# Turning the quantised input of a feed-forward block by transposing DMA transfers instead of TensorE transposes, in a fused macaron block

## The reference

```python
def ffn(x):                                   # weights w_gate, w_up (704 x 256), w_down (256 x 704)
    gate, y = fp4_linear(x, w_gate), fp4_linear(x, w_up)
    return fp4_linear(silu(gate) * y, w_down)
# fp4_linear: both operands quantised in blocks of 16 to the grid 0, .5, 1, 1.5, 2, 3, 4, 6
#             times a scale per block, then einsum('bsk,nk->bsn')
x = x + 0.5 * ffn(layernorm(x))               # A
x = x + scan_block(layernorm(x))              # S: 16 states for each of the 256 channels
x = x + 0.5 * ffn(layernorm(x))               # C
```

## Time and profile before

| | |
|---|---|
| median of 3 runs | 4089.68 us (4085.27 to 4096.99) |
| profiled execution, its own time | 4087.75 us |
| its span | 4085.6 us |
| lies around the span | 2.15 us |
| TensorE busy, share of the span | 3666.8 us, 90% |
| VectorE busy | 3519.3 us, 86% |
| ScalarE busy | 3020.7 us, 74% |
| GpSimd busy | 2700.2 us, 66% |
| mean granted TensorE clock | 0.962 |

### The profile page before, as it was taken

How to read it: one execution, slowest core, us unless ns; L and a number is a source line. 1 busy time by engine, 2 the same in 40 slices (tenths; PEclk the granted TensorE clock), 3 DMA queues, 4 the chain that set the end, 5 groups by cost and what they waited for, 6 DMA issues and landing times. The chain is left out here.

```text
span 4085.6 us, 81699 instructions
## 1 busy us (share of the span) xinstructions
PE 3666.8 (90%) x29740; PEld 2764.4 (68%) x29740; DVE 3519.3 (86%) x5974; ACT 3020.7 (74%) x5991; POOL 2700.2 (66%) x2163
## 2 busy tenths in 40 slices
...
GB/s 29 11 11 17 6 17 12 17 17 17 11 13 12 17 17 17 17 6 17 12 17 17 17 6 17 12 17 17 17 17 6 12 17 16 17 17 6 12 12 11
DMA packets 46452, 57.93 MB, mean 14 GB/s; under 512 B 7463, under 2 KB 41704, under 8 KB 46056
## 3 DMA queue, kind: packets, MB, share of 16 engines
q1 hardware_dynamic: 46056, 52.72, 3.9%
...
...
## 5 line engine op out<-in xcount | busy, mean ns | idle before, releaser
L803 DVE TENSOR_TENSOR_SCAN state<-w_ps,decay 128x512 f32<-128x512 f32 x1024 | 1211.4, 1211 | 31.2 <-PE w_ps L1192 20.1
L1126 PE MATMUL gu_ps<-wgu,qxT 128*128 128x352 f16 x6144 | 1064.1, 324 | 181.9 <-DVE hid L730 139.4
L1126 PEld LDWEIGHTS gu_ps<-wgu,qxT 128*128 128x128 f16 x6144 | 579.4, 100 | 616.9 <-DVE hid L730 188.3
L1192 PE MATMUL w_ps<-bdif,x_parts 128*128 128x129 f16 (+1 forms) x12288 | 846.5, 221 | 24.6 <-DVE state L803 21.1
L1192 PEld LDWEIGHTS w_ps<-bdif,x_parts 128*128 128x128 f16 x12288 | 767.2, 98 | 98.6 <-issue 53.2
L813 DVE SCALAR_TENSOR_TENSOR c_state<-state,inv_A,rep_ps 128x512 f32<-128x512 f32 x1024 | 726.4, 736 | 13.8 <-PE y_ps L1212 10.1
L1133 PE MATMUL td_ps<-wd,qhT 128*128 128x256 f32 x3072 | 728.6, 388 | 4.2 <-ACT qhT L926 4.2
L1005 ACT ACTIVATE decay<-dt,A_sb 128x512 f32<-128x512 f32 x1024 | 679.0, 714 | 4.9 <-DVE state L803 3.1
L995 ACT ACTIVATE bdif<-dif,B_tok 128x129 f16<-128x129 f16 x2048 | 637.3, 397 | 5.2 <-PE w_ps L1192 1.0
L1133 PEld LDWEIGHTS td_ps<-wd,qhT 128*128 128x128 f32 x3072 | 575.7, 194 | 78.5 <-ACT qhT L926 6.8
L926 ACT COPY qhT<-td_ps 128x256 f32<-128x256 f32 x768 | 282.0, 367 | 443.4 <-PE td_ps L1107 438.4
...
## 6 DMA issues: line engine op xcount, KB each, us to landing
x_in<-in_L_attn_x SPq DMA_DIRECT2D x32, 512.0 KB, 3.7
x_s<-x_a SPq DMA_DIRECT2D x32, 512.0 KB, 2.9
out<-x_out SPq DMA_DIRECT2D x32, 512.0 KB, 2.8
...
```

Of the source, the lines that this page charges most:

```text
L803: v.tensor_tensor_scan(state[:, n % 2, gi, :], w_ps[:, gi, :], decay[:, n % 2, gi, :], 0.0, ALU.add, ALU.mult).then_inc(state_ready.sem, 1)
L1126: last = te.matmul(gu_ps[:, m, 0:FH], qxT[:, t // 2, 4 * (t % 2) + xp * G + c], wgu[:, c, wp, a:a + FH], start=begin, stop=end)
L1192: last = te.matmul(w_ps[:, gi, t * P:t * P + wide], x_parts[:, xp, t, gi * P:(gi + 1) * P], bdif[:, n % NB, t, bp, 0:wide], start=(t, xp, ...
```

## The change

The matmuls of `tx` and the copies behind them are gone. SyncE issues, for each half, one transposing DMA transfer from `qx` to `qxT` (both in SBUF, 256 KB), and has a list of its own in `ORDER`. `qx` is laid out anew (tokens outside the two parts), so that each half is one stretch. The first `gu` of a pass waits for the first half alone, the fifth for the second. The lists of TensorE, VectorE, ScalarE and GpSimd hold the same entries as before except `tx`, in another order.

```diff
+    "SP": """
+    S.keep0 C.tx0 C.tx1 N.load0 N.tx0 N.tx1 C.store0
@@
-        qx = sb("qx", [P, 2, T, DM], F16)
+        qx = sb("qx", [P, T, 2, DM], F16)
@@
+            def turn_x(q, pair):
+
+                sp.wait_ge(qx_ready.sem, qx_ready.at(q, 2 * pair + 2))
+                if not first(q):
+                    sp.wait_ge(gu_ready.sem, gu_ready.at(q - 1, 8 * pair + 8))
+                sp.dma_start_transpose(qxT[:, pair], qx[:, 2 * pair:2 * pair + 2].rearrange("p t a k -> p (t a k)")
+                                       ).then_inc(tx_out[pair].sem, 16)
@@
-            def take_x(q, pair):
-                act.wait_ge(tx_full.sem, tx_full.at(q, pair + 1))
-                if not first(q):
-                    act.wait_ge(gu_ready.sem, gu_ready.at(q - 1, 8 * pair + 8))
-                a.copy(qxT[:, pair], x_bank(pair)).then_inc(tx_out.sem, 1)
@@
-            def transpose_x(q, pair):
-                pe.wait_ge(qx_ready.sem, qx_ready.at(q, 2 * pair + 2))
-                if not first(q):
-                    pe.wait_ge(hid_ready.sem, hid_ready.at(q - 1, 2 * T))
-                for t in range(2):
-                    for part in range(2):
-                        for c in range(G):
-                            last = te.transpose(x_bank(pair)[:, 4 * t + 2 * part + c],
-                                                qx[:, part, 2 * pair + t, c * P:(c + 1) * P], ident16[:])
-                last.then_inc(tx_full.sem, 1)
@@
-                    if k == 0:
-                        pe.wait_ge(tx_out.sem, tx_out.at(q, 2))
-                    elif m == 0:
-                        pe.wait_ge(silu_ready.sem, silu_ready.at(q, k))
-                    else:
+                    if m == 0:
+                        if k % T == 0:
+                            pe.wait_ge(tx_out[k // T].sem, tx_out[k // T].at(q, 16))
+                        if k:
+                            pe.wait_ge(silu_ready.sem, silu_ready.at(q, k))
+                        elif not first(q):
+                            pe.wait_ge(silu_ready.sem, silu_ready.at(q - 1, 2 * T))
+                    elif k:
                         pe.wait_ge(hid_ready.sem, hid_ready.at(q, k))
+                    elif not first(q):
+                        pe.wait_ge(hid_ready.sem, hid_ready.at(q - 1, 2 * T))
```

More of the change, by code:

```diff
@@ L28 @@
     "PE": """
[L29 to L33, removed]
@@ L37 @@
+    C.ht11 S.p28 S.p29 C.dn3 S.p30 S.p31
     """,
     "DVE": """
[L39 to L46, removed]
+    S.ln0 A.hid0 C.ln0 A.hid1 A.am0 A.hid2 C.xa0 C.xa1 C.xs0 A.hid3 A.am1 A.qs0 S.cb0 A.hid4 S.tb0 S.sc0 C.xm0
@@ new lines @@
+    S.k0 A.qm0 S.k1 A.hid5 S.dt0 A.hid6 A.am2 C.qy0 A.qm1 S.g0 S.g1 A.hid7 S.p0 S.g2 S.p1 A.am3 A.res0 S.g3 S.p2
+    S.p3 A.qs1 C.xm1 S.g4 S.g5 S.p4 S.p5 S.g6 S.g7 C.qy1 A.qm2 C.hid0 S.g8 S.g9 C.hid1 S.p6 S.p7 C.am0 C.hid2
+    A.res1 S.g10 C.hid3 A.qm3 S.p8 S.p9 S.g11 C.am1 S.p10 S.p11 S.g12 S.g13 S.p12 C.qs0 C.hid4 S.p13 S.g14 S.g15
+    A.res2 C.qm0 C.qm1 S.p14 S.p15 C.hid5 S.g16 S.g17 S.p16 S.p17 C.hid6 C.am2 S.g18 S.g19 C.hid7 C.am3 S.p18
+    C.qs1 A.res3 S.p19 S.g20 S.g21 N.ln0 S.p20 S.g22 C.qm2 C.res0 S.p21 S.g23 S.g24 C.qm3 S.p22 S.p23 S.g25
```

83 lines of the change are left out of this document (43 added, 40 removed).

## The result

The changed kernel takes **3956.96 us** (median of 4 runs, 3953.13 to 3962.2) where the kernel before takes 4090.75 us beside it on the same chip: 0.9673 times the time, 95% interval 0.9653 to 0.9693, 134 us less. The forecast was 67 us less. The profiled execution is one of 3953.13 us, with a span of 3951.0 us.

What follows compares the result with a forecast made beforehand. TensorE was taken to bound the full stretches, a dependency chain the middle one. 1.98 + 0.32 = 2.3 us over 31 iterations, 71 us, less 4 for filling and draining, gave 4023 us; 8-in-10 range 3972 to 4105.

Steps and rivals of the forecast that it cites:

- the rest of the middle stretch at zero: In the 35.30 us from S.ln0 to the first scan, reordering beyond C.xm0 was counted as no gain.
- rival 3: A longer idle time and less filler double TensorE's slow-clock spell of 1.9 us per iteration: 4080 us, chance 0.09.
- The longer idle time of 2.9 us: TensorE's idle time before gu 7 was to grow to 1.92 + 0.96 = 2.9 us, covered by the chain.
- TensorE's matmuls: Removing the transposes of C and N was to take 1.98 us per iteration from TensorE's full stretches.
- 0.63 us for C's first half: Gain where C's first half was turned: 0.98 us, plus 0.61 of empty gap between the ht, less 0.96 for two e.
- ScalarE's copies: Four removed copies of 1.01 us were counted as nothing, since ScalarE has 27 us idle per iteration.
- The first scan: Moving hidden piece 7 and x_magic behind it gains nothing: TensorE's full stretch, not that scan, sets the pace.
- `C.xm0` behind `CB`: In the middle stretch, this reordering was to pull the chain forward by 0.32 us per iteration.
- The landing: A transposing transfer was to land in 5.1 us (1024 packets at 55 ns, plus 1.6), with ends 2.2 and 88.
- The cover: After N.qy0, TensorE reaches A.gu0 in 5.1 us; a transfer may take 7.1 before anything but TensorE waits.
- Rival 1: A late transfer at A.gu0 costs landing less 7.1 us per iteration; at 12 us 4174 us, chance 0.17.
- Rival 2: VectorE, idle 5.5 us in the full stretches, becomes the bound; only 0 to 1 us won, 4060 to 4090, chance 0.12.

Runs made afterwards that it cites:

- e3: The changed kernel with GpSimd's C.xv1 put back directly behind C.xv0, as before: 3999.91 us, ratio 0.978 to the kernel before.
- e5: The kernel before with only GpSimd's C.xv1 moved behind A.mv1, no transposing transfers: 4040.55 us, ratio 0.9886 to the kernel before.
- e4: The changed kernel with A.hid7 put back ahead of the first scan on VectorE: 3961.16 us, ratio 0.9673 to the kernel before.
- e1: The changed kernel, with transposing transfers, but the four old lists less their tx entries: 4098.83 us, ratio 1.0028 to the kernel before.
- e8: The changed kernel with TensorE's order of the middle stretch as before: 3975.48 us, ratio 0.9709 to the kernel before.
- e6: The changed kernel with 8 idle matmuls at each place where TensorE turned x before: 4001.12 us, ratio 0.9765 to the kernel before.
- e7: The changed kernel with a 128x1024 fp16 copy on ScalarE at each place of the old copies: 3958.43 us, ratio 0.9669 to the kernel before.
- e12: The changed kernel with C.xm0 ahead of CB again and ScalarE's C.ax0 ahead of A.gu4: 3963.14 us, ratio 0.968 to the kernel before.
- e9: The changed kernel with VectorE's N.qy0 put behind the last residual, directly ahead of N.qy1: 4066.0 us, ratio 0.994 to the kernel before.
- e2: The kernel before with the new lists, tx put back on TensorE and ScalarE, C.qy1 two scans earlier: 4174.48 us, ratio 1.0206 to the kernel before.

## Why the prediction was wrong in size

**The step that failed** is the reordering: "I leave the rest of the middle stretch at zero". With the 0.32 us of my sum, the stretch lost 2.4 us per iteration. 1.3 to 1.4 of them are the stall of VectorE's scale step beside GpSimd's second product, 43 us by e3 and 47 by e5. Another 0.6 us are hidden piece 7, which e4 shows to be no gain: it only moves from the middle stretch into the full one. I read TensorE's and VectorE's idle times in that stretch, and the stall is in none: it is a busy row 1.55 us long beside three others of the same form with 0.2. The groups by line would have pointed at it, with 519 ns in the mean over 128 of them where one takes 200; after the change the mean is 206:

```profile
L743 DVE TENSOR_SCALAR scale<-amax 128x88 f32<-128x88 f32 x128 | 66.4, 519 | 2.3
```

```profile
L753 DVE TENSOR_SCALAR scale<-amax 128x88 f32<-128x88 f32 x128 | 26.3, 206 | 1.2
```

(Groups by line of VectorE before, then after: total busy us and mean ns, then idle us ahead of it.) I had "VectorE and GpSimd keep all their work" and left it there, where one entry of GpSimd's list counts as much as all the matmuls that were taken away.

**TensorE's clock** was left out of the sum, and rival 3 gave it the wrong sign. The rival had it that a longer idle time and less filler make the slow spell longer. e1 shows that this does happen with the transfers alone, and takes what gain is left there. But the new list moves the spell into time in which TensorE is waited for by nobody; by e8 that is 15 to 18 us. The longer idle time of 2.9 us did not come: with the two `w` ahead of them, the last two groups of `gu` wait 1.61 and 1.85 us. The 1.9 us that I gave for a spell is near what the runs show (0.9 us in the mean full stretch of before against its fast ones, 2.4 in the slow ones of e8, 3 in those of e1).

**TensorE's matmuls**: forecast 1.98 us, measured 1.2 to 1.6 (e6). The mechanism holds. That the whole full stretch became 1.9 us shorter, close to the 1.98, is luck: part of it is the clock, for between full stretches at 1.00 the difference is 1.1 us, and hidden piece 7 and an `x_magic` step came in from the middle. The term was a start-to-start difference at three places, and one of them, 0.63 us for C's first half, rested on gaps that the order of e1 leaves open instead. (The lower end of my range, "N's and C's second half", should read 1.35 us and not 1.2; nothing hangs on it.)

**ScalarE's copies**: zero, and zero it is (e7). **The first scan**: it has slack, as said (e4). **`C.xm0` behind `CB`**: 0.32 us forecast, 0.2 measured (e12).

**The landing**: 5.1 us taken, 3.1 measured, 3.0 to 4.6. The count of packets was right: (181224 - 46056) over 128 transfers are 1056 for each, against 1024. The 55 ns for a packet were too much: by the queue's shares of the two pages, 8.7% of 16 times 3951.0 us less 3.9% of 16 times 4085.6, over 135168 packets, it is some 22 ns (an estimate), and with the 1.6 us of the earlier trace rows that gives the 3.1. The cover (5.1 us for TensorE) held in either case. The estimate from the Trainium skill's "VectorE: DVE Perf Modes", by which eight blocks one after another take 10.5 us, does not hold: the measurement decides, and 256 KB in 3.1 us is near the 2.9 us of a copy of twice the size. Rival 1 did not happen; but e9 shows what it costs with `N.qy0` directly ahead of `N.qy1`: 109 us at a landing of 3.2. Rival 2 did not happen: VectorE idles 2.7 us in the full stretch after and TensorE 0.8.

**The account.** Of 134 us, by the medians: the stall 43, the matmuls 44, TensorE's order in the middle stretch 18, `C.xm0` 6, copies and hidden piece 7 nothing that can be told. 23 us are not singled out. By the ratios it is 44, 38, 15 and 3, and 34 are left; each of these differences has an interval of some 10 us to either side. What is left may lie in entries that moved within the full stretch, and in `N.qy0` and `N.qy1`, whose old places make the transfer late and the adding wait (e1); no run puts these back alone at both places. These are prices at the changed kernel, each with all the rest in place. They don't add up from the other end, as e1 shows: the transfers alone are worth nothing, and the one placing of the new order without them that was run (e2) is slower than the kernel before. So the transfers need the order; whether the order needs the transfers is not shown, since e2 put the turning where its product waits. For one entry, `C.xv1`, e5 shows that it does not: 47 us without a transfer. Which of the remaining entries bring the last 23 to 34 us stays open. No run was faster than the changed kernel by more than the noise.
